# Forward transforms of context attention over half-length sums and differences, one table load per Gelu, new order of work

## What is computed

```python
Qf = jnp.fft.rfft(Q, axis=2)
Kf = jnp.fft.rfft(K, axis=2)
corr = jnp.fft.irfft(Qf * jnp.conj(Kf), n=Lloc, axis=2)
corr_mean = corr.mean(axis=-1)
w, idx = jax.lax.top_k(corr_mean, top_k)
w = jax.nn.softmax(w, axis=-1)
# then the sum over the top k of w times V rolled by idx, and an output projection
```

## Time and profile before

| | |
|---|---|
| median of 3 runs | 1030.68 us (1026.15 to 1031.63) |
| the profiled execution's own time | 1032.04 us |
| its span, first to last instruction | 1030.3 us |
| TensorE busy | 911.1 us, 88% |
| VectorE busy | 792.5 us, 77% |
| ScalarE busy | 565.7 us, 55% |
| mean granted TensorE clock | 0.963 |

### The profile page before, as it was taken

One profiled execution on the slowest core, in us unless ns is written; L12 is line 12 of the kernel. 1 busy time (PEld: TensorE's weight loads), 2 busy tenths in 40 slices (PEclk: granted clock), 3 DMA queues, 4 the chain that ended last, 5 costly groups with the idle time before them and its releaser, 6 DMA issues.

```text
span 1030.3 us, 11040 instructions
## 1 busy us (share of the span) xinstructions
PE 911.1 (88%) x3719; PEld 553.9 (54%) x3738; DVE 792.5 (77%) x1301; ACT 565.7 (55%) x902; POOL 44.7 (4%) x112
## 2 busy tenths in 40 slices
PE   0489945889999999989998999989999999999795
PEld 0145623555575647654766457644766476647345
DVE  3778799778987899779987799779988997183141
ACT  0566674487428564767457553885467745421410
POOL 0000100100001000100010000100010002000000
PEclk9889986999999999999998999999999999999899
DMA  5900100010002000110001000200002000000000
GB/s 153 239 1 1 62 0 0 21 42 1 1 14 69 1 1 1 43 41 1 1 21 61 1 1 1 83 1 0 1 1 62 1 1 21 1 0 1 21 1 21
DMA packets 39082, 25.48 MB, mean 25 GB/s; under 512 B 18647, under 2 KB 38642, under 8 KB 39026
## 3 DMA queue, kind: packets, MB, share of 16 engines
q1 hardware_dynamic: 39026, 24.77, 8.6%
HBM read 20.57 MB, written 4.19 MB: 24 GB/s over the span
## 4 chain that ended last, share of the span: by engine, by line
PE 64%; DVE 15%; ACT 13%; issue 5%; SPq 1%; POOL 1%; DMA 0%; ACTq 0%; DVEq 0%; POOLq 0%
PE ps L811 9%; PE ps L792 9%; PE ps L783 9%; PE ps L672 7%; PE ps L610 4%; PE ps L595 3%; PE ps L640 3%; PE ps L716 3%; PE ps L463 3%; PE ps L656 3%; DVE zc L2460 2%; PE ps L726 2%; DVE sc L2539 2%; ACT x L1674 2%; ACT L1422 1%
## 5 line engine op out<-in xcount | busy, mean ns | idle before, releaser
L2539 DVE TENSOR_TENSOR_SCAN sc<-mask,sc 128x1024 f32<-128x1024 bf16 x64 | 146.3, 2285 | 0.5
L783 PE MATMUL ps<-cum,mw 128*128 128x512 f32 x256 | 121.9, 598 | 3.2 <-ACT cs L1669 2.9
L792 PE MATMUL ps<-x2t,mv 128*128 128x512 f32 x256 | 121.6, 597 | 1.6 <-DVE prod L2767 0.7
L811 PE MATMUL ps<-up,prod 128*128 128x256 f32 x512 | 116.2, 380 | 1.3 <-DVE prod L2767 0.9
L811 PEld LDWEIGHTS ps<-up,prod 128*128 128x128 f32 x512 | 95.1, 190 | 15.9 <-issue 3.8
L1669 ACT ACTIVATE cs<-ps 128x512 f32<-128x512 f32 x64 | 37.9, 592 | 102.4 <-PE ps L783 98.1
L2460 DVE SCALAR_TENSOR_TENSOR zc<-ps,cw,zc 128x510 f32<-128x510 f32 (+2 forms) x96 | 71.3, 743 | 22.7 <-ACT zc L1484 20.3
L2531 DVE TENSOR_TENSOR sc<-sc,g 128x1024 f32<-128x1024 f32 x64 | 77.7, 1214 | 9.7 <-ACT sc L1555 9.6
L1573 ACT ACTIVATE sq<-sc 128x1024 f32<-128x1024 f32 x48 | 50.4, 1050 | 58.7 <-DVE acc L2551 58.7
L783 PEld LDWEIGHTS ps<-cum,mw 128*128 128x128 f32 x256 | 47.3, 190 | 58.8 <-issue 56.2
L595 PE MATMUL ps<-xt,win 128*128 128x512 f32 x128 | 66.7, 650 | 9.5 <-DVE zc L2460 9.5
(11 more groups left out here) (263 smaller groups left out, 1551.6 us busy)
## 6 DMA issues: line engine op xcount, KB each, us to landing
xa<-in_x_dram SPq DMA_DIRECT2D x8, 512.0 KB, 3.5
xs_a<-in_x_dram SPq DMA_DIRECT2D x8, 512.0 KB, 3.8
cin<-in_ctx_dram SPq DMA_DIRECT2D x8, 512.0 KB, 5.6
out_dram<-prod SPq DMA_DIRECT2D x8, 512.0 KB, 4.8
prod<-in_L_ffn_V_fwd_dram SPq DMA_DIRECT2D x2, 256.0 KB
prod<-in_L_ffn_W_fwd_dram SPq DMA_DIRECT2D x2, 256.0 KB
prod<-in_L_ffn_W_inv_exp_dram SPq DMA_DIRECT2D x2, 256.0 KB
prod<-in_L_ffn_V_inv_dram SPq DMA_DIRECT2D x2, 256.0 KB
```

Source lines behind the costliest of these rows:

```text
L783: last = mm(o, mw[:, t, br, c:c + P], cum[:, t, :], start=(t == 0), stop=(t == 1))
L792: last = mm(o, mv[:, t, br, c:c + P], x2t[:, t, :], start=(t == 0), stop=(t == 1))
L811: mm(d, prod[:, j, q * P:(q + 1) * P], up[:, j, :], start=(j == 0), stop=False)
L2539: V.tensor_tensor_scan(flat, mask[:, 0:2 * T], flat, 0.0, ALU.mult, ALU.add)\
```

## The change

- TensorE's `b_transform` no longer adds up two token halves. VectorE first forms, for the context and for x1, the sum and the difference of the two token halves (`b_fold`, new, two operations over 128x1024 each). Even frequencies need only the sum, odd ones only the difference, so each matmul has the 128 columns of one parity and starts and ends its own group. The number of calls stays, so 32 matmuls a chunk.
- The context's sum and difference are written over `cin` in place; those of x1 go over `xs_a`, whose content has been used by then. The next load of the residual therefore waits for the transform "xf" instead of the norm.
- The constants hold the frequencies in the order even, then odd.
- `c_hidden` asks for the table set that holds Gelu.
- The lists of calls of all engines are written anew. The folds of the context stand near `a_weight`, those of x1 after the second `a_conv` of the next chunk. ScalarE's list groups the four `c_hidden` of a chunk more closely. B's later steps (`b_corr`, `b_topk`, `b_wt`, `b_apply`, `b_back`, `b_out`) come later within a chunk than before, in several chunks behind C's output products. TensorE's list for chunk 0 has fold(0) ahead of `a_spread(0, 0)`.

The diff, cut to its core (the lists by three short extracts):

```diff
-EXP_LN, SILU_SIN = "natural_log_exp_and_others", "silu_and_others"
+EXP_LN, SILU_SIN, GELU = "natural_log_exp_and_others", "silu_and_others", "gelu_and_others"
...
+        xh = xs_a[:, :, :].rearrange("p (b h) d -> p h b d", h=2)
+        ch = cin[:, :, :].rearrange("p (b h) d -> p h b d", h=2)
...
             def load_residual(i):
                 if not is_first(i):
-                    sp.wait_ge(*ACT_A.at(i - 1, "norm", NQ - 1))
+                    sp.wait_ge(*PE_B.at(i - 1, "xf", 1))
...
             def b_transform(i, name, t):
-                src = cin if name == "cf" else x1
-                if name == "cf":
-                    pe.wait_ge(ctx_loaded, 16 * i + 16)
-                else:
-                    pe.wait_ge(*ACT_A.at(i, "norm", NQ - 1))
+                src = ch if name == "cf" else xh
+                pe.wait_ge(*VEC_B.at(i, "fold", 1 if name == "cf" else 3))
                 o = free_b(i, name, t)
                 for b in range(SEQ):
+                    d = o[:, b * L:(b + 1) * L].rearrange("p (a h k) -> p h a k", a=2, h=2)
                     for h in range(2):
-                        last = mm(o[:, b * L:(b + 1) * L], src[:, 2 * b + h, t * P:(t + 1) * P],
-                                  fdft[:, h, :], start=(h == 0), stop=(h == 1))
+                        last = mm(d[:, h, :, :], src[:, h, b, t * P:(t + 1) * P],
+                                  fdft[:, 0, :].rearrange("p (a h k) -> p h a k", a=2, h=2)[:, h, :, :], start=True, stop=True)
...
             def c_hidden(i, n):
-                tables(SILU_SIN)
+                tables(GELU)
...
+            def b_fold(i, name):
+                if name == "cf":
+                    dve.wait_ge(ctx_loaded, 16 * i + 16)
+                    TT(ch[:, 1, :, :], ch[:, 0, :, :], ch[:, 1, :, :], ALU.subtract).then_inc(*VEC_B.tick("fold", 0))
+                    dve.wait_ge(*VEC_B.at(i, "fold", 0))
+                    STT(ch[:, 0, :, :], ch[:, 0, :, :], 2.0, ch[:, 1, :, :], ALU.mult, ALU.subtract).then_inc(*VEC_B.tick("fold", 1))
+                else:
+                    x = x1[:, :, :].rearrange("p (b h) d -> p h b d", h=2)
+                    dve.wait_ge(*ACT_A.at(i, "norm", NQ - 1))
+                    TT(xh[:, 0, :, :], x[:, 0, :, :], x[:, 1, :, :], ALU.add).then_inc(*VEC_B.tick("fold", 2))
+                    TT(xh[:, 1, :, :], x[:, 0, :, :], x[:, 1, :, :], ALU.subtract).then_inc(*VEC_B.tick("fold", 3))
...
             a_weight(0)
+            b_fold(0, "cf")
             a_factor(0)
...
             a_conv(1, 1)
+            b_fold(0, "xf")
             a_fraction(1, 0)
...
+            b_fold(1, "cf")
             a_weight(1)
```

More of the change, by code:

```diff
@@ L105 @@
 POOL_B = Steps("pool_b", each("rstd", range(4)))
-VEC_B = Steps("vec_b", ["aabb", "ab", "ba", "heads", "ca", "cb0", "cb1", "cb2", "corr", "top", "negmax",
+VEC_B = Steps("vec_b", each("fold", range(4)) + ["aabb", "ab", "ba", "heads", "ca", "cb0", "cb1", "cb2", "corr", "top", "negmax",
                         "above", "equal", "order", "first", "also", "keep", "weight", "inv", "wn",
@@ L406, in _ @@
             load_ctx(2)
+            store(0)
+            load_residual(3)
             load_x(4)
-            load_residual(3)
-            store(0)
             load_ctx(3)
+            load_ctx(4)
+            store(1)
+            load_residual(4)
             load_x(5)
-            load_residual(4)
-            store(1)
-            load_ctx(4)
+            store(2)
             load_x(6)
             load_residual(5)
-            store(2)
             load_ctx(5)
+            store(3)
             load_x(7)
+            load_ctx(6)
             load_residual(6)
-            store(3)
-            load_ctx(6)
-            load_residual(7)
             store(4)
             load_ctx(7)
+            load_residual(7)
             store(5)
@@ L820, in _ @@
             a_project(0, 1)
+            fold(0)
             a_spread(0, 0)
@@ L824, in _ @@
             a_project(0, 3)
-            fold(0)
+            a_sums(0, 0)
             fold(1)
@@ L943, in _ @@
             c_running(0, 3)
+            b_spectrum(1, "ka")
+            b_spectrum(1, "kb")
+            b_spectrum(1, "va")
+            b_spectrum(1, "vb")
             c_spread(0, 3)
@@ L1062, in _ @@
             a_project(4, 2)
+            b_spectrum(3, "qa")
+            b_spectrum(3, "qb")
+            b_spectrum(3, "ka")
+            b_spectrum(3, "kb")
             c_logits(2)
@@ L1734, in _ @@
             a_angles(0, 5)
-            fold(13)
+            a_turns(0, 7)
+            a_squares(0, 3)
+            a_angles(0, 6)
+            a_squares(0, 4)
             fold(14)
@@ L1752, in _ @@
             fold(25)
+            fold(26)
             a_squares(0, 5)
-            fold(26)
+            a_squares(0, 6)
+            a_squares(0, 7)
             fold(27)
@@ L1757, in _ @@
             fold(29)
-            a_squares(0, 6)
-            a_squares(0, 7)
+            fold(30)
             a_norm(0)
             a_transpose(1, 0)
-            a_transpose(1, 1)
-            fold(30)
             fold(31)
             fold(32)
+            a_transpose(1, 1)
             fold(33)
@@ L2276, in _ @@
             b_exp(7)
-            b_wt(7)
             c_tile(6, 5)
@@ L2332, in _ @@
             rstd(1, 0, VEC_A, POOL_A)
+            rstd(0, 2, VEC_C, POOL_C)
             rstd(1, 1, VEC_B, POOL_B)
-            rstd(0, 2, VEC_C, POOL_C)
             rstd(2, 0, VEC_A, POOL_A)
@@ L3408, in shape_constants @@
     c[0:HD, C_E8:C_E8 + P] = np.arange(HD)[:, None] == p[None, :] % HD
-    t, f = np.arange(L)[:, None], np.arange(P)[None, :]
+    order = np.concatenate([np.arange(0, P, 2), np.arange(1, P, 2)])
+    t, f = np.arange(L)[:, None], order[None, :]
     ang = 2.0 * np.pi * ((t * f) % L) / L
@@ L3413, in shape_constants @@
     fwd[:, P] = (-1.0) ** np.arange(L)
-    scale = np.where(np.arange(P) == 0, 1.0, 2.0)[:, None] / L
+    scale = np.where(order == 0, 1.0, 2.0)[:, None] / L
     inv = np.stack([fwd[:, 0:P].T * scale, fwd[:, P:].T * scale])
```

944 lines of the change are left out of this document (473 added, 471 removed).

## The result

The changed kernel takes 993.71 us (median of 4, 993.26 to 994.34) against 1028.81 for the kernel before on the same chip: ratio 0.9659, 95% interval 0.9627 to 0.9691. The forecast was 1019 us, 1003 to 1042: the side was right, the size was not, by 25 us. The profiled execution took 994.34 us.

What follows compares the result with a forecast made beforehand. It took TensorE to set the pace from 193 us on, VectorE only 9 points behind in the steady stretch, and VectorE before that. Sum: 1032.0 - 14 + 3.5 - 1 = 1020.5, less 1.4 for the median: 1019 us, range 1003 to 1042.

Steps and rivals of the forecast that it cites:

- The spacing of 128-column matmuls: Transforms on TensorE: products 0.112 us apart in place of 0.216, saving 3.3 us a chunk, 26.6 in all.
- the other queues: Weight, residual and store queues and POOL: the changed order of loads and steps there was priced at nothing.
- Rival (4): Transforms on TensorE: load and columns don't overlap at 128 columns, 0.219 us apart, nothing saved: 1043 us; chance 0.07.
- The folds: VectorE's sums and differences of token halves: 4.9 us a chunk, 39 us in all, making VectorE 832 us busy.
- the start: Stretch from 104 to 193 us, VectorE setting the pace: folds only partly covered by waits, +3.5 us.
- TensorE's idle time in the steady stretch: Six chunks, 193 to 861 us: TensorE's work falls 20.0 us, its idle time grows one microsecond a chunk: -14 us.
- A microsecond taken from TensorE is worth a microsecond: From 193 us to the end, TensorE's savings count in full, only while VectorE has room for added work.
- The table loads: ScalarE: 54 loads in place of 65, 14.1 us less, priced at nothing of its own since ScalarE isn't the bound.
- The end: From 861 us: last chunk's transforms save 3.3 us, its x fold adds to TensorE's wait for the normalisation; net -1.
- (1): Steady stretch: the order fills VectorE's waits entirely, -20 there, 1009 us in all; chance 0.20.
- (2): Steady stretch: the folds eat up what TensorE gives, the stretch stays 668 us, 1033 us in all; chance 0.17.
- (3): Steady stretch: VectorE sets the pace and its listed waits stay, +16.7 there, 1053 us in all; chance 0.11.

Runs made afterwards that it cites:

- the run with 44 calls: Kernel after with 44 calls of idle products (twice the matmuls intended, 9.99 us) in TensorE's 6.0 us wait ahead of the last chunk's transposes: 995.15 us, ratio 0.9656.
- the run with 14.4 us behind the folds: Kernel after with an extra 0.9 us VectorE operation, result unread, behind each fold's result, 14.4 us in all: 1002.98 us, ratio 0.9763.
- the halves alone: Kernel before with half-length transforms and their folds put into its old lists, old table set kept: 1045.63 us, ratio 1.0144.
- order without halves: Kernel after with the transforms of before and no folds, so new order and Gelu's own table set: 1019.34 us, ratio 0.9903.

## Why the prediction was wrong

**Right.** The spacing of 128-column matmuls: a run of 16 takes 1.95 us, (1.95 - 0.28) / 15 = 0.111 us, and the transforms are busy 16.3 + 16.1 = 32.4 us, as forecast. 54 table loads, none at the Gelu line. No cost on the other queues: in the trace of after no engine waits for a load after the start. Rival (4), load and columns one after the other, is refuted by the 0.111 us.

The Trainium skill, TensorE: Matmul & The Clock Gate, section Part 3: Packing small matmuls, says in one sentence that a load overlaps only matmuls of another row group; with full groups the run shows otherwise. The same section also lets a load that goes to the background weight buffer be pulled ahead, which the prediction left out; the run doesn't show which buffer is used.

**The folds, a term of the sum that was mis-sized.** I wrote "three tensor-tensor operations and one scalar-tensor-tensor over 128x1024 f32", 39 us. The trace has four over 128x512 (two sequences of 256 channels each), 0.68 to 0.70 us, 2.7 us a chunk and 22 in all; the section on the change has the same slip. VectorE is busy 811.8 us, not 832. In the sum the size enters directly at the start: with the durations measured the context fold of chunk 0 fits its wait of 1.38 us and the x fold costs 1.4, so the forecast would have been +1.4 in place of +3.5, with -0.3 measured. (The second chunk begins 2 us later than before and makes it up; 1 to 2 us is also scatter there, since the run with 44 calls, the same up to that point, has its third chunk at 190.9 us.) How much of the rest hangs on it can only be estimated: by the run with 14.4 us behind the folds, at 9.3 us of time, 17 us more of VectorE would have cost 11 us, less than half of the 25.

**TensorE's idle time in the steady stretch, the step that failed.** I set one microsecond more a chunk, "set, not derived"; it fell by 1.9 a chunk. That is 17.6 us, less the 1.8 us by which busy time fell short (18.2 for 20): 15.8 of the miss. The fold size above is part of it, since I had set the idle time with 4.9 us of folds a chunk in mind. Two things were missed. First, the order was costed only as cover for the folds, though alone it gives 10 us: in the five chunks TensorE's idle time is 23.2 us before and 11.3 with the order alone (545.10 less 533.79). The halves on top of it leave the idle time where it is (11.8 and 10.8), so the growth by the folds that I had added did not come. Second, with fewer waits the granted clock in the five chunks is 1.00 for 0.99, and TensorE's busy time 3 us less for the same products.

**"A microsecond taken from TensorE is worth a microsecond"** held in the new order (26.9 of 28.6) and was false in the one that I read it from: there 27 us fewer were worth nothing. 96% busy was no proof of a bound. Had the order been left as it was, nothing in the forecast's sum would have changed but the cover for the folds; without the order 1037 us came out, and 1046 without the table set too. What bounds the old order is shown mainly by exclusion: it is neither engine's amount of work. Two runs point at the waits themselves, since 8 table loads fewer gave 7 us there and the same work in another order gave 10. The exact ring of waits stays open.

**The table loads, priced at nothing.** They give 6 to 7 us in three of the four settings and nothing in the fourth, order without halves (0.9896 and 0.9903). TensorE waits for the Gelu's result, a row on ScalarE at 55% busy (3.0 us in the five chunks without the set, 0.3 with it, in the new order with halves): the busy share hid a latency. Why it is worth nothing in the fourth setting is not shown; TensorE's listed waits for that row are there only 1.8 us without the set.

**The end.** Forecast -1, measured -7.3. The x fold of chunk 7 was to add to TensorE's wait for the norm; there is no such wait any more. From the eighth chunk's transposes to the end it is 277.6 us before, 278.0 with the order alone, 277.9 with the halves alone, 271.6 with both and 270.1 with the table set too. So the columns show there only in the new order (64 matmuls, 6.7 us, against the 6.4 seen), and the table set gives 1.5.

**The rivals.** (1), the order fills the waits, was the right mechanism with too small a price: it took the idle time as unchanged at best, and nothing in it let idle time fall. (2), the folds eat the gain, is what the old order does, and worse. (3) didn't come, but VectorE has little left: 14.4 us more of it cost 9 to 11.

## What to carry to other kernels

Before pricing work taken off an engine in a schedule of strict lists, ask whether the engine is bound by its amount of work or by when its inputs come; a share of 96% doesn't tell, a run with that engine's work doubled or taken away at one place does. An order and an edit must be priced together: the same edit cost 1.4% in one order and gave 2.4% in the other. Read the shape of a new operation from the tile it works on before multiplying its duration by anything.

## What the runs showed of the hardware

**Some stalls cost TensorE twice.** In the old order with halves, granted clock by stretch around the 4.36 us wait:

```profile
540.00:547.00 7.00, 7.00 (x21) 3.17 (x19) 4.38 (x13) 6.96 (x12) 1.56 (x4) 1.00 0.00 1
547.20:551.70 4.50, 0.15 (x1) 0.00 (x0) 3.48 (x6) 2.01 (x4) 0.00 (x0) 0.80 0.00 0
551.70:555.50 3.80, 3.79 (x17) 3.79 (x18) 1.05 (x2) 1.67 (x3) 0.00 (x0) 0.50 0.00 0
```

Full clock (2.4 GHz) up to the wait, then 0.50, its lower level of 1.2 GHz, for the matmuls behind it: 3.78 us for 1.95. The same 16 matmuls in two other chunks of that run, behind shorter waits, and the clock granted to them:

```profile
328.65 2.05 PE L656 MATMUL ps<-fdft,xs_a 128*128 128x128 f32 x16 [2.23 <-DVE xs_a L2618]
672.13 3.26 PE L656 MATMUL ps<-fdft,xs_a 128*128 128x128 f32 x16 [3.43 <-DVE xs_a L2618]
```

```profile
328.60:330.70 2.10, 2.05 (x16) 1.86 (x16) 2.06 (x4) 2.10 (x4) 0.00 (x0) 1.00 0.00 0
672.10:675.40 3.30, 3.27 (x17) 3.27 (x18) 0.64 (x1) 0.60 (x1) 0.00 (x0) 0.60 0.00 0
```

Behind the wait of 2.23 us the clock stayed at 1.00, behind that of 3.43 us it was mostly the lower one. Filling the 5.99 us wait at the end of after with products that nobody reads kept the clock at 1.00 and brought 2 us.

**GpSimd can hold up VectorE.** A sum or difference of 128x512 f32 took GpSimd 1.3 us at the place shown and 1.50 and 1.57 in the mean, for VectorE's 0.68, and a VectorE cast beside it took 1.15 us for 0.20. Not every operation is held up: beside the next fold a scalar-tensor-tensor of the convolution, with one input in PSUM, took 0.74 us, its usual time. The Trainium skill, SBUF — State Buffer, section Terms, says that both share a port pair which one instruction holds for its whole length while the other is blocked; the cast's row agrees.
